# Four experts' second matmuls summed in one accumulator, with the hidden units weighted on VectorE, in a four-layer transformer kernel on one core

## What is computed

```python
gate_logits = xf @ w_gate
topk_logits, topk_idx = jax.lax.top_k(gate_logits, TOP_K)
gates = jax.nn.softmax(topk_logits, axis=-1)
cw = jnp.sum(jax.nn.one_hot(topk_idx, NUM_EXPERTS, dtype=xf.dtype) * gates[..., None], axis=1)
hmid = jax.nn.gelu(jnp.einsum('tc,ech->eth', xf, w1) + b1[:, None, :], approximate=True)
eo = jnp.einsum('eth,ehc->etc', hmid, w2) + b2[:, None, :]
moe = jnp.einsum('te,etc->tc', cw, eo).reshape(B, N, C)
return x + g_mlp[:, None, :] * moe
```

## Time and profile before

| | |
|---|---|
| median of 3 runs | 1643.86 us (1642.82 to 1645.86) |
| the profiled execution's own time | 1644.07 us |
| its span, first to last instruction | 1642.2 us |
| PE busy | 1493.4 us (91%) |
| DVE / ACT / POOL busy | 936.9 / 800.9 / 532.8 us |
| mean granted TensorE clock | 0.951 |
| starts of the eight groups of `mlp(0)` on PE | 256.38, 303.57, 348.03, 392.49, 437.83, 487.25, 534.02, 583.42 us |

### The profile page before, as it was taken

One profiled execution on the slowest core, in us unless ns is written; L12 is line 12 of the kernel. 1 busy time (PEld: TensorE's weight loads), 2 busy tenths in 40 slices (PEclk: granted clock), 3 DMA queues, 4 the chain that ended last, 5 costly groups with the idle time before them and its releaser, 6 DMA issues. The chain is left out here.

```text
span 1642.2 us, 41566 instructions
## 1 busy us (share of the span) xinstructions
PE 1493.4 (91%) x16128; PEld 1094.8 (67%) x16128; DVE 936.9 (57%) x2410; ACT 800.9 (49%) x1431; POOL 532.8 (32%) x739
## 2 busy tenths in 40 slices
PE   6789899999999998989899878886999799998998
PEld 2466676777777775666677656665677567666776
DVE  4688872323232325788636679887446466565442
ACT  2366663233323334666645456665544265554543
POOL 3345532111121211554332423343325144332331
PEclk9799999999999999999999878998999699999999
DMA  4765630000020200565200334344116667776021
GB/s 129 153 139 137 146 86 24 15 15 15 8 73 1 73 8 25 146 130 124 57 24 23 87 92 109 100 108 106 29 37 82 107 93 105 122 120 103 16 64 45
DMA packets 209316, 126.23 MB, mean 77 GB/s; under 512 B 143921, under 2 KB 192656, under 8 KB 203938
## 3 DMA queue, kind: packets, MB, share of 16 engines
q1 hardware_dynamic: 189162, 121.00, 34.1%
q10 hardware_dynamic: 19960, 2.57, 1.2%
HBM read 89.56 MB, written 33.18 MB: 75 GB/s over the span
## 5 line engine op out<-in xcount | busy, mean ns | idle before, releaser
L1100 ACT ACTIVATE prob<-banks 128x1024 f32<-128x1024 f32 x256 | 262.0, 1024 | 227.3 <-PE banks L620 226.4
L1381 DVE TENSOR_REDUCE negm<-banks 128x8 bf16<-128x1024 f32 x256 | 311.3, 1216 | 92.0 <-PE banks L598 89.1
L1222 ACT ACTIVATE hid<-banks 128x512 f32<-128x512 f32 x280 | 166.6, 596 | 354.5 <-PE banks L862 353.4
L879 PEld LDWEIGHTS banks<-wfc,hid 128*128 128x128 f32 (+1 forms) x2240 | 289.0, 193 | 12.5 <-issue 9.7
L879 PE MATMUL banks<-wfc,hid 128*128 128x144 f32 (+1 forms) x2240 | 295.7, 290 | 0.2 <-DVE gx L1411 0.2
L861 PE MATMUL banks<-hT,wfc 128*128 128x512 f32 x560 | 291.7, 602 | 0.5 <-ACT hid L1222 0.5
L1723 POOL TENSOR_TENSOR X<-X,gx 128x288 f32<-128x288 f32 x128 | 100.6, 799 | 463.8 <-DVE gx L1411 461.6
L862 PE MATMUL banks<-hr,rfc 66*128 66x512 f32 x280 | 225.9, 807 | 0.0
L598 PE MATMUL banks<-qk 54*128 54x128 bf16 (+1 forms) x2048 | 125.0, 244 | 70.7 <-DVE negm L1381 40.2
L616 PE MATMUL banks<-qk 54*128 54x128 bf16 (+1 forms) x2048 | 171.7, 238 | 6.6 <-ACT prob L1100 5.6
L631 PE MATMUL banks<-prob,V 128*32 128x128 f32 x4096 | 172.9, 289 | 2.4 <-ACT OT L1106 2.4
(11 more groups left out here) (148 smaller groups left out, 2263.0 us busy)
## 6 DMA issues: line engine op xcount, KB each, us to landing
qk<-qk_scr SPq DMA_DIRECT2D x336, 72.0 KB
gbuf<-gate_scr SPq DMA_DIRECT2D x64, 288.0 KB, 3.9
qk_scr<-parts SPq DMA_DIRECT2D x48, 288.0 KB, 2.7
qk<-qk_scr SPq DMA_DIRECT2D x48, 216.0 KB
qk<-tok_scr SPq DMA_DIRECT2D x112, 72.0 KB
qk_scr<-parts SPq DMA_DIRECT2D x48, 144.0 KB, 2.4
qk<-qk_scr SPq DMA_DIRECT2D x48, 144.0 KB
tok_scr<-parts SPq DMA_DIRECT2D x48, 96.0 KB, 4.7
```

Of the source, the lines that this page charges most:

```text
L879: mm = pe.matmul(bank[4 + q][:, C * (b % 2):C * (b % 2) + C], hid[0:rows, t, T * b:T * b + T], wfc2[0:rows, k, t, :], start=(t == 0), stop ...
L1100: act.activation(prob[:, 2 * (U % 2):2 * (U % 2) + 2, :], pairs[1][:], ACT.Exp, scale=scale).then_inc(a_exp, 1)
L1222: act.activation(hid[0:rows, t, :], bank[2 + i % 2][0:rows, :], func).then_inc(a_gelu, 1)
L1381: dve.tensor_reduce(negm[:, u // 2, :, 4 * (u % 2):4 * (u % 2) + 4], pairs[0][:].rearrange("q s (h k) -> q s h k", k=T), AX.X, ALU.max, ne ...
```

## The change

The hidden units themselves are multiplied by the expert's weight, on DVE between GELU and the second matmul, so that all experts' second matmuls of a group add up in the same banks. Two experts' last 64 units share a tile (18 tiles in a group, not 20; the columns of `w1` and `b1` of experts 1 and 3 are rolled by 64 on the host, and a fifth tile holds units of two experts). The second matmuls of a tile stand three tiles (`BEHIND`) behind its first ones. Because the hidden units lie on the partitions and the tokens along the row, the weights are needed as a row that is the same on all partitions: SP writes `cw` to DRAM turned (`cw_scr`) and reads it back to all 128 partitions (8 KB each) into a free part of `qk` (`spread_weights`). So `cw` of a group is made a group earlier (`gate_logits(g + 1)` behind tile 9, `top2` in four parts, `powers` on POOL); that of group 0 in the last group of the attention. The biases `b2` are weighted apart (`biases`) and added at the end (`add_biases`). What stood after a sequence or an expert now stands after a tile. The other layers' MLPs keep their instructions.

```diff
+TILES = [(e, t) for e in range(E) for t in range(KT - 1 + e % 2)]
+NT = len(TILES)
+BEHIND = 3
...
+        def gates_by_row(g):
+            room = qk[:, 0, 2] if g == 0 else qk[:, (g - 1) % 2, 1]
...
+            def spread_weights(g):
+                sp.wait_ge(d_cw, CR + 16 * (g + 1))
+                if g >= 2:
+                    sp.wait_ge(q_gw, 16 * (g - 1))
+                sp.dma_start(cw_scr[g % 2].rearrange("e b t -> t (e b)"), cw_t[:].rearrange("t e b -> t (e b)"),
+                             allow_slow_non_contiguous=True).then_inc(q_cww, 16)
...
+                sp.wait_ge(q_cww, 16 * (g + 1))
+                sp.dma_start(gates_by_row(g).rearrange("p e t -> p (e t)"),
+                             cw_scr[g % 2].rearrange("e b t -> (e b t)").unsqueeze(0).to_broadcast([128, E * TG])) \
+                    .then_inc(q_gw, 16)
...                SP, attention(0), last group
+                    if l == 0 and g == 7:
+                        spread_weights(0)
...                SP, mlp(0), in each group, behind write_parts and read_parts
+                    if l == 0 and g < 7:
+                        spread_weights(g + 1)
...                PE
+                def expert_first(g, j, h):
+                    i, (e, t) = NT * g + j, TILES[j]
+                    at = HID * e + 128 * t + TAIL * (e % 2) if t < KT - 1 else HID * e - TAIL
+                    w, x = (a[:, at:at + 128] for a in (wfc1_t, rfc1_t))
+                    pe.wait_ge(a_gelu, CR + i - 1)
+                    pe.matmul(bank[2 + i % 2][:], w, hT[:, h, :], start=True, stop=False)
+                    pe.matmul(bank[2 + i % 2][:], x, hr[:, h, :], start=False, stop=True).then_inc(s_fc1, 1)
+                def expert_second(g, j):
...
+                        pe.matmul(bank[4 + q][:, 0:2 * C], pick[:, 0, :], pick[:, 1:4, 0:2 * C // 3], start=True, stop=False)
+                    pe.wait_ge(d_hg, CR + i + 1)
+                    for b in range(G):
+                        mm = pe.matmul(bank[4 + b // 2][:, C * (b % 2):C * (b % 2) + C], hid[:, i % KT, T * b:T * b + T],
+                                       wfc2[:, e - (t == KT - 1), t, :], start=False,
+                                       stop=(j == NT - 1 and b % 2 == 1))
...
+                def expert_step(g, h):
+                    for j in range(NT):
+                        expert_first(g, j, h)
+                        if j < KT:
+                            after_tile(g, j)
+                        if j >= BEHIND:
+                            expert_second(g, j - BEHIND)
+                        if g < 7 and j in (5, 7, 9, 11):
+                            after_seq(g, (j - 5) // 2)
...
+                        if g < 7 and j == 9:
+                            gate_logits(g + 1, 0)
+                        if g == 7 and j >= NT - AHEAD:
...
+                            scores_for_max(l + 1, UNITS * N + j - NT + AHEAD)
+                    for j in range(NT - BEHIND, NT):
+                        expert_second(g, j)
...                DVE
+                def weighted(g, j):
+                    i, (e, t) = NT * g + j, TILES[j]
+                    dve.wait_ge(a_gelu, CR + i + 1)
+                    if j == 0:
+                        dve.wait_ge(q_gw, 16 * (g + 1))
...
+                        x = hid[:, i % KT, :]
+                        ins = dve.tensor_tensor(x, x, w[:, e, :], ALU.mult)
+                    ins.then_inc(d_hg, 1)
...
+                def expert_step(g):
+                    for j in range(NT):
+                        weighted(g, j)
+                        if g == 0 and j == 0:
+                            normed(4 * N - 1)
...
+                        if b0 <= j < b0 + E:
+                            biases(g, j - b0)
...
+                        if g in (4, 6) and j in (9, 11, 13):
+                            m = (j - 9) // 2
+                            rest1(N + nxt, m, 6 if m == 1 else 7)
+                        if g < 7 and j in (10, 11, 12, 15):
+                            top2(g + 1, min(j - 10, 3), 0)
...                POOL, mlp(0)
+                    for m in range(3):
+                        if l == 0 and g < 7 and m == 2:
+                            powers(g + 1)
+                        if l in (0, 2) and g in (4, 6):
                             parts23(N + (g - 4) // 2, m)
```

More of the change, by code:

```diff
@@ L664, in project, with gate_logits @@
                 mm.then_inc(s_pj, 1)
+            def gate_logits(g, o):
+                k = 8 + g
+                h = slot_of(k)
+                if g:
+                    pe.wait_ge(d_top, CR + 2 * g)
+                else:
+                    pe.wait_ge(q_wg, 16)
+                    pe.wait_ge(d_ws, CR + 3)
+                wait_normed(k)
+                for b in range(G):
+                    out, at = bank[o][:, E * b:E * b + E], slice(T * b, T * b + T)
+                    pe.matmul(out, hT[:, h, at], wgate[:], start=True, stop=False)
+                    mm = pe.matmul(out, hr[0:REM - 2, h, at], rgate[:], start=False, stop=True)
+                mm.then_inc(s_lg, 1)
             def start_layer(l):
@@ L855, in mlp @@
                 pe.wait_ge(a_exp, CR + 8 * N)
[L857 to L868, removed]
+                def first(f0, h, t):
+                    i, at = f0 + t, HID * (l - 1) + 128 * t
+                    pe.wait_ge(a_gelu, CR + i - 1)
+                    pe.matmul(bank[2 + i % 2][:], wfc1_t[:, at:at + 128], hT[:, h, :], start=True, stop=False)
+                    pe.matmul(bank[2 + i % 2][:], rfc1_t[:, at:at + 128], hr[:, h, :], start=False, stop=True) \
+                        .then_inc(s_fc1, 1)
@@ L882, in second @@
                         mm.then_inc(s_y, 1)
[L884 to L892, removed]
                 def turn(k, i6, i7):
@@ L1001, in mlp @@
                     if l == 0:
[L1002 to L1010, removed]
-                            if e == (E - 1 if l == 0 and g == 7 else 0):
-                                after_seq(g, b)
-                        if g == 0 and e == 0:
-                            project(l, N - 1, 0, 6)
-                            project(l, N - 1, 1, 7)
+                        expert_step(g, h)
+                        continue
+                    f0 = fc1_base[l] + KT * g
+                    for t in range(KT):
+                        first(f0, h, t)
+                        after_tile(g, t)
+                    for b in range(G):
+                        second(g, f0, b)
+                        after_seq(g, b)
+                    if g == 0:
+                        project(l, N - 1, 0, 6)
+                        project(l, N - 1, 1, 7)
                 if l == 1:
@@ new lines, in mlp @@
+                for g in range(8):
+                    if l == 0:
+                        expert_step(g)
+                        continue
+                    f0 = fc1_base[l] + KT * g
+                    for t in range(KT):
+                        i, rows = f0 + t, min(128, HID - 128 * t)
+                        act.wait_ge(s_fc1, CR + i + 1)
+                        if t == 0:
+                            act.wait_ge(s_y, CR + y_base[l] + 2 * g)
+                        act.activation(hid[0:rows, t, :], bank[2 + i % 2][0:rows, :], func).then_inc(a_gelu, 1)
+                        after_tile(g, t)
+                    after_tiles(g)
@@ new lines, in biases @@
+                def biases(g, e):
+                    if e == 0 and g == 0:
+                        dve.wait_ge(q_b2, 16)
+                        dve.wait_ge(s_ont, CR + N)
+                        dve.wait_ge(g_ox, CR + N)
+                    if e == 0:
+                        dve.wait_ge(d_cw, CR + 16 * (g + 1))
+                        if g:
+                            dve.wait_ge(d_gate, CR + 2 * (m0 + g))
+                    else:
+                        dve.wait_ge(d_bi, CR + E * g + e)
+                    for b in range(G):
@@ L1580, in mlp @@
                         rest1(N + (g - 5) // 2, 0, 6)
-                    if l == 0:
-                        for q in range(2):
-                            experts(g, 0, q)
                     for k in prepared_mlp(l, g):
@@ L1589, in mlp @@
                             gated(m0 - 1, q, pair_of(6 + q))
-                    if l == 0:
-                        for e in range(1, E):
-                            if g == 7 and e == E - 1:
-                                first_maxima()
-                            for q in range(2):
-                                experts(g, e, q)
-                        dve.wait_ge(d_y, CR + Y_OF[0] * (g + 1))
                     if l == 2 and g == 7:
@@ L1754, in attention @@
                     prepare(turned_at(l, g + 1) if g < 6 else 16 * l + 8 + g - 4)
+                    if l == 0 and g == 7:
+                        powers(0)
             def mlp(l):
```

253 lines of the change are left out of this document (176 added, 77 removed).

## The result

The changed kernel takes **1711.49 us** (median of 4 runs, 1708.02 to 1728.15) against 1644.86 us before (1642.82 to 1646.73): a ratio of 1.044, 95% interval 1.0399 to 1.0481. (The ratios given here are those on record; they can differ by some tenths of a per cent from the quotient of the medians, which is 1.0405 here.) It is slower, as forecast, but by 67 us and not by 16, and outside the range. The profiled execution took 1712.88 us, with a span of 1711.1.

A forecast was written before the change was run, and what follows sets the result against it. PE was taken to bound `mlp(0)`. From 1644.07 us: group 0 +11, net work -28, gate logits -2, ordinary stalls +4, groups 5 and 7 +27, clock +9, end -5: +16, 1660 us (1645 to 1680; over all 1632 to 1692).

The forecast's parts named there:

- The new path to the weights: From finished `cw` through DRAM write, read and first weighting to released PE: 11.3 us (9 to 18), write 4.2.
- the stall terms: PE waiting for weights in `mlp(0)`: 0.8 us in groups 1, 2, 3, 4, 6 (+4); 13.7 in 5 and 7 (+27).
- the clock term: PE at 1.2 GHz for about 6 us behind each of three long stalls, 3 us each: +9.
- group 0: Start of `mlp(0)`: late power and first weighting delay PE's `on_main` from 263.00 to 276.1; net +11 us.
- PE work of groups 1 to 7: 18 tiles instead of 20 in `mlp(0)`: net work -28 us, group 7's gate logits -2.
- behind the stage: After the last second matmul of `mlp(0)`: less DVE work before first scores, -4 us, and clock -1: -5.
- PE's prices: In `mlp(0)`: first tile 1.09 us, a tile's second matmuls 0.98; clean group 40.5 us.
- Rival C: DVE becomes the bound in tiles 5 to 8, stalling 1 us in each group: 1668 us; chance 0.08.
- Write and read: Weights' DRAM write of 4-byte pieces 4.2 us (2.4 to 8), 1 MB read 6.2 us (5.5 to 9).
- Groups 5 and 7: Weights' write queues behind query and key parts' reads in groups 4 and 6: stall 13.7 us each, +27.
- The order that I assumed: Each DMA engine serves a queue in order, so write waits behind parts' reads: 13.7 us stall, not 8.3.
- rival B: 4-byte pieces are dear: write takes 8 us, eight stalls grow by 3.8 (+30), 1690 us or more; chance 0.13.

The follow-up runs named there:

- experiment 2: Changed kernel with weights written and read for groups 0 and 1 only, groups 2 to 7 weighting with group 1's rows: 1634.85 us, ratio 0.996.
- experiment 3: Changed kernel with SP issuing the weights' transfers ahead of the parts' in groups 4 and 6: 1691.96 us, ratio 1.0278.
- experiment 1: Changed kernel with the 8 KB write as 128 pieces of 64 bytes instead of 2048 of 4, weights in another order: 1648.33 us, ratio 1.004.
- experiment 4: Changed kernel, 4-byte pieces spaced 16, 32, 64 or 256 bytes apart, read taking `x` instead: 1668.7, 1658.2, 1655.01 (ratio 1.0069), 1654.4 us.
- 5: Changed kernel with the weights transposed on TensorE, copied out by ScalarE and written as 16 pieces of 512 bytes: 1651.13 us, ratio 1.0048.

## Why the prediction was wrong

The step that failed is one term of "The new path to the weights": **"I take 4.2" for the write, which took 10.6**. The range that I gave it ended at 8, "five times the price for each piece"; I had priced what the packets cost, and the time lies behind them. With that, and with the clock that fell behind every stall and not behind three, the stall terms and the clock term were too small: of the 53 us that the forecast misses, 33 are stalls, 14 the clock and 7 group 0. The table sets the forecast against the profiled execution (us against before; the group starts are 268.43, 324.58, 373.04, 422.64, 472.06, 524.86, 587.94 and 640.51, the last second matmul ends at 703.63, against 631.04 before):

| | forecast | measured | how |
|---|---|---|---|
| group 0, clock included | +14 | +21.0 | 324.58 - 303.57 |
| PE work of groups 1 to 7 | -30 | -32.0 | groups without stall: 40.51, 40.51, 41.39, 43.8, 42.82, 43.79, 42.71, against 327.47 |
| stalls of groups 1 to 7 | +31 | +63.9 | the row of waits |
| clock in groups 1 to 7 | +6 | +19.7 | 379.05 - 295.5 - 63.9 |
| behind the stage | -5 | -3.7 | rest of the spans |
| sum | +16 | +68.9 | 1712.88 - 1644.07 = 68.8 |

(The lengths without stall are those of experiment 2; for group 1 that of group 2, and for group 4, where one profile shows 0.96, the 43.8 of group 6, which has the same extra work.)

- **PE's prices were right.** Forecast 40.5 us for a clean group, measured 40.51.
- **DVE.** A weighting takes 0.695 us (forecast 0.65), DVE is busy for 26 to 28 us of a plain group. Rival C is out: in experiment 2 no group without a fetch waits for DVE.
- **Write and read.** Write 10.6 instead of 4.2, read 5.1 instead of 6.2: the path is 5.3 us longer. The five ordinary stalls are 5.7 us on average instead of 0.8, 4.9 more: the mis-sized term accounts for them.
- **Groups 5 and 7.** 17.6 instead of 13.7. The order that I assumed holds: with SP's order alone changed both fall to an ordinary stall (experiment 3), and in group 5's trace the small write's packets come behind the reads', landing after 14.1 us. With 64 bytes between the pieces, where the write does land in 4.2, these stalls measured 14.3 and 14.1.
- **The clock.** I had it fall in three long stalls, at 3 us each. It fell in all seven of groups 1 to 7, and each costs 1.7 to 3.7 us on top: 48.46 - 40.51 - 6.27 = 1.7 in group 1, 3.7 in group 6, where it fell once more behind the gate logits (at 618 us). The long ones cost no more than the ordinary ones, 2.7 and 2.8. I named this under rival B and gave it no price.
- **Group 0.** The place was right (`on_main`, behind the first weighting). It comes at 284.53 instead of 276.1: 5.3 from the path, the rest from an attention that ended late in this execution. The power starts at 263.88, not at 260.4, and the first write is issued at 267.7; in the kernel of experiment 1, which has the same code up to there, it is issued at 262.4.
- **The end.** -3.7 for -5, but one profile can't tell them apart: behind the last second matmul the kernels of experiments 1, 2, 4 (at 64 bytes) and 5, which have the same instructions there, took 1000.1 to 1008.0 us, against 1007.5 for the change and 1011.2 for before.

The check of the whole model is the kernel of experiment 4 with 64 bytes between the pieces: it has the landing that I had assumed, and came out at 1.0069 times before, where the forecast of 1660 is 1.0097, within 5 us. Some of that is luck. In its profile (1647.70 us) the stalls are 28.4 us where the forecast had 31, but group 0 costs 7.5 us and not 14, the clock 10.8 and not 6, and the rest is 11 us shorter and not 5. The direction was right, and rival B was the nearest case ("1690 us or more"); I had given it 0.13, too little, because the only argument against it, quick 64-byte pieces, was one on packets. The Trainium skill, "DMA: Bandwidth & Descriptors", section "Anatomy of one DMA — SWDGE (gpsimd) path", says of DMAs that GpSimd issues that most of their fixed cost of about 2 us is the wait until the last byte is confirmed in the target memory, which can be surprisingly long where that is HBM. This write is on SP's queue, and its trace agrees on where the time lies, behind the last packet, but not on how much it is: over 7 us. The rule of the Trainium skill on transfers under 512 B (same page, "Specifications"), which I had cited for rival B, does not by itself explain it: 64-byte pieces landed in 1.4 us. Why the landing is so late when neighbours lie within 32 bytes, no run here shows.

## What to carry to other kernels

A small DMA that turns a tile by writing single elements is to be priced by its landing, not by its packets or bytes; if no row shows such a landing, it is the first thing to measure. Here elements from different partitions that become neighbours in DRAM were the dear case: turn the tile on TensorE first and write whole rows. And a latency paid once in every group counts with the number of groups and again in the clock behind each stall, so put such transfers ahead of bulk traffic on their queue and make their data a few tiles sooner.

## What the runs showed of the hardware

- The landing of 2048 writes of 4 bytes to DRAM depends on their distance: 10.6 us at 4 bytes, 6.1 at 16, 4.5 at 32, 4.2 at 64, 3.9 at 256. The same 8 KB as 128 pieces of 64 bytes lands in 1.4 us, as 16 pieces of 512 bytes in 1.3.
- TensorE's granted clock can fall to 0.5 with PE busy all the time: behind 17 of 49 patches of 1.95 us of matmuls of only 4 columns, at a cost of 1.65 to 1.7 us where nothing else disturbs the group. In two halves, 2.1 to 3.2 us of other matmuls apart, none of seven did it in the one profile taken; that this is more than chance is likely and not shown.
- Behind an idle stretch of PE of 5.1 to 6.3 us the clock was at 0.5 as it was behind one of 17.6, and cost about as much (1.7 to 3.7 us, and 2.7 to 2.8).
